# Turning the attention weights in two halves of query rows, in the attention loop of a graph network kernel

## The reference

```
q = (x @ Wq + bq).reshape(n, heads, C)      # heads = 2, C = 64
k = (x @ Wk + bk).reshape(n, heads, C)
v = (x @ Wv + bv).reshape(n, heads, C)
alpha = sum(q[dst] * k[src], axis=-1) / sqrt(C)
ex = exp(alpha - segment_max(alpha, dst)[dst])
a = ex / segment_sum(ex, dst)[dst]
out = segment_sum(v[src] * a[..., None], dst).reshape(n, heads * C)
return out + x @ Ws + bs
```

## Time and profile before

| | us |
|---|---|
| median of three runs | 2256.75 |
| the profiled execution, time | 2258.27 |
| the profiled execution, span | 2256.3 |
| TensorE busy | 2103.7 (93% of the span) |
| VectorE busy | 1578.7 (70%) |
| ScalarE busy | 1292.8 (57%) |

### The profile page before, as it was taken

How to read it: one execution, slowest core, us unless ns; L and a number is a source line. 1 busy time by engine, 2 the same in 40 slices (tenths; PEclk the granted TensorE clock), 3 DMA queues, 4 the chain that set the end, 5 groups by cost and what they waited for, 6 DMA issues and landing times. The chain is left out here.

```text
span 2256.3 us, 55086 instructions
## 1 busy us (share of the span) xinstructions
PE 2103.7 (93%) x19640; PEld 1706.4 (76%) x19640; DVE 1578.7 (70%) x4061; ACT 1292.8 (57%) x2303; POOL 834.2 (37%) x1091
## 2 busy tenths in 40 slices
PE   1299999999999999999997999999999999999998
PEld 1288888898888888988885677777776577777776
DVE  1457888888788887887773666666664666667665
ACT  1166666665666666666663455656654455655555
POOL 0765777677667767776730000000000000000000
PEclk9599999999999999999998999999999999999999
DMA  4001111111111111111112122222220222222220
GB/s 121 14 31 46 42 46 51 42 42 46 54 40 46 45 51 39 50 50 44 40 45 98 66 79 86 85 85 85 85 85 33 86 92 93 92 92 92 92 92 7
DMA packets 52537, 141.55 MB, mean 63 GB/s; under 512 B 9261, under 2 KB 43755, under 8 KB 45855
## 3 DMA queue, kind: packets, MB, share of 16 engines
q1 hardware_dynamic: 49804, 129.55, 16.2%
q0 software_dynamic: 2576, 9.68, 1.6%
HBM read 93.95 MB, written 45.27 MB: 62 GB/s over the span
## 5 line engine op out<-in xcount | busy, mean ns | idle before, releaser
L776 PE MATMUL ps<-matrixT,x_rows 125*128 125x256 f32 (+1 forms) x2500 | 581.6, 383 | 2.8 <-ACT aggT L862 2.1
L843 ACT COPY matrixT<-ps 125x500 f32<-125x500 f32 (+2 forms) x800 | 395.7, 582 | 224.7 <-PE ps L764 220.7
L776 PEld LDWEIGHTS ps<-matrixT,x_rows 125*128 125x128 f32 x2500 | 459.8, 190 | 71.3 <-issue 3.2
L1466 ACT COPY weightsT_l<-ps 125x500 f32<-125x500 f32 (+1 forms) x450 | 234.0, 543 | 368.9 <-PE ps L1387 368.9
L764 PE MATMUL ps<-high_weights,low_onehot 64*125 64x125 f32 x6300 | 404.6, 279 | 23.6 <-issue 11.7
L1544 DVE CUSTOM_DVE_ANT_0 scores_l<-ps,bias_rows_l 125x500 f32<-125x500 f32 (+1 forms) x700 | 396.8, 619 | 35.3 <-issue 33.7
L764 PEld LDWEIGHTS ps<-high_weights,low_onehot 64*125 64x125 f32 x6300 | 367.0, 189 | 53.5 <-issue 31.9
L1387 PEld LDWEIGHTS ps<-eye,scores_l 125*125 125x125 f32 x2500 | 301.0, 189 | 115.7 <-issue 97.3
L1387 PE MATMUL ps<-eye,scores_l 125*125 125x125 f32 x2500 | 364.1, 286 | 4.7 <-ACT scores_l L1448 3.4
L1552 DVE COPY weightsT_l<-ps 125x500 f32<-125x500 f32 (+1 forms) x250 | 150.0, 600 | 267.3 <-PE ps L1387 264.9
L1448 ACT ACTIVATE scores_l<-scores_l,neg_max_l 125x1500 f32<-125x1500 f32 x200 | 320.9, 1605 | 20.5 <-DVE neg_max_l L1581 20.2
(11 more groups left out here) (154 smaller groups left out, 2028.1 us busy)
## 6 DMA issues: line engine op xcount, KB each, us to landing
bias_rows_l<-bias SPq DMA_DIRECT2D x50, 1562.5 KB, 6.6
bias<-bias SPq DMA_DIRECT2D x150, 250.0 KB, 2.0
edges<-rec POOLq DMA_DIRECT2D x1, 2014.2 KB, 11.8
x_rows<-in_x SPq DMA_DIRECT2D x1, 1562.5 KB
bias<-bias SPq DMA_DIRECT2D x25, 62.5 KB, 1.6
x<-x_rows SPq DMA_DIRECT2D x25, 62.5 KB
x_rows_l<-x SPq DMA_DIRECT2D x25, 62.5 KB
out<-rows_l SPq DMA_DIRECT2D x25, 62.5 KB
```

The source lines that it names most:

```text
L776: last = nc.tensor.matmul(psG[:, BASES * SPLIT * side:BASES * (SPLIT * side + SIDE[side])], x[:, h, :], MT[side][:, 0:SIDE[side], BASES * ...
L843: last = nc.scalar.copy(MT[side][:, at:at + 2 * c - 1:2, 0:COLS], psP[bank][0:R, :].rearrange("p (i c) -> p i c", c=128)[:, 0:c, 0:COLS])
L1466: nc.scalar.copy(PT[i % 8][:, 0:cw[c]], psT[i % 2][0:R, 0:cw[c]]).then_inc(z["pa_ok"], 1)
```

## The change

`turn` now handles a chunk of both heads in one call. Each block of 125 query rows by 125 source nodes is transposed in two parts: rows 0 to 63 (`QS[0]`, 64 rows) into bank `psT[0]`, rows 64 to 124 (61 rows) into bank `psT[1]`. A full chunk is 16 transposes in place of 8. The first of each chunk is written as a matmul with the identity and not as a transpose. A bank holds both heads of a chunk (8 parts of 64 or of 61 columns). The copies now take one bank each: i = 2c + side in place of 2c + head, still on the same engines, and they wait on one count of `t_ps` per chunk. The eight `PT` tiles of one head become four of both heads. Lines 1405 and 1406 (1420 and 1421 in the changed kernel) move ahead of the turn of chunk 2s-2, so that they come straight behind the products.

```
         QS = ((0, HD), (HD, R))

-            def turn(u, up, i):
-                c, hd = i // HEADS, i % HEADS
+            def turn(u, up, c):
                 if c in (0, EXP_AT):
-                    pe.wait_ge(z["exp_ok"], u * 4 + (hd + 1 + 2 * (c > 0)))
-                if i >= 2:
-                    chunk_out(pe, u, i - 2)
-                elif not is_int(u) or u >= 1:
-                    chunk_out(pe, u - 1, i - 2 + NT)
-                for b in range(cw[c] // R):
-                    n = 4 * c + b
-                    last = nc.tensor.transpose(psT[i % 2][0:R, b * R:(b + 1) * R], S[up][:, hd, n * R:(n + 1) * R],
-                                               eye[0:R, 0:R])
+                    pe.wait_ge(z["exp_ok"], u * 4 + (2 if c == 0 else 4))
+                for i in (HEADS * c - 2, HEADS * c - 1):
+                    if i >= 0:
+                        chunk_out(pe, u, i)
+                    elif not is_int(u) or u >= 1:
+                        chunk_out(pe, u - 1, i + NT)
+                k = cw[c] // R
+                for hd in range(HEADS):
+                    for b in range(k):
+                        at = (4 * c + b) * R
+                        for side, (lo, hi) in enumerate(QS):
+                            n = hi - lo
+                            to = psT[side][0:R, (hd * k + b) * n:(hd * k + b + 1) * n]
+                            if hd == 0 and b == 0 and side == 0:
+                                nc.tensor.matmul(to, S[up][lo:hi, hd, at:at + R], eye[lo:hi, lo:hi], start=True, stop=True)
+                            else:
+                                last = nc.tensor.transpose(to, S[up][lo:hi, hd, at:at + R], eye[lo:hi, lo:hi])
                 last.then_inc(z["t_ps"], 1)

+        def turned_chunk(eng, u, i):
+            c, (lo, hi) = i // HEADS, QS[i % HEADS]
+            k = cw[c] // R
+            eng.wait_ge(z["t_ps"], u * CH + (c + 1))
+            buffer_free(eng, u, i)
+            return (PT[c % 4][:, :, 0:k, lo:hi],
+                    psT[i % HEADS][0:R, 0:HEADS * k * (hi - lo)].rearrange("p (h b q) -> p h b q", h=HEADS, b=k))
...
-                                                PT[(HEADS * c + hd) % 8][:, b * R:(b + 1) * R],
+                                                PT[c % 4][:, hd, b, :],
```

More of the change, by code:

```diff
@@ L1239, in conv @@
         S = [sb(f"scores{i}", [R, HEADS, NODES], F32) for i in range(2)]
-        PT = [sb(f"weightsT{i}", [R, CW], F32) for i in range(8)]
+        PT = [sb(f"weightsT{i}", [R, HEADS, 4, R], F32) for i in range(4)]
         mx = [sb(f"chunk_max{i}", [R, HEADS, CH], F32) for i in range(2)]
@@ L1267, in conv @@
         EXP_BEFORE = {2: 2, 4: 3}
+        QS = ((0, HD), (HD, R))
         EXP_AT = 3
@@ L1398, in step @@
                         product(w, par, CH - 1)
-                    if s > 0 and inside(u):
-                        turn(u, up, 4 * s - 4)
-                        turn(u, up, 4 * s - 3)
                     if s == 2 and inside(w):
@@ L1406, in step @@
                         nc.tensor.matmul(psO[par][0:R, 384:384 + D], x_now[par][:, :], W["s"][:, :], start=True, stop=True).then_inc(z["o_ps"], 1)
+                    if s > 0 and inside(u):
+                        turn(u, up, 2 * s - 2)
                     if s > 0 and inside(t):
@@ L1411, in step @@
                     if s > 0 and inside(u):
-                        turn(u, up, 4 * s - 2)
-                        turn(u, up, 4 * s - 1)
+                        turn(u, up, 2 * s - 1)
                         if s == 1 and (not is_int(u) or u >= 2):
@@ L1422, in step @@
                 if inside(u):
-                    turn(u, up, NT - 2)
-                    turn(u, up, NT - 1)
+                    turn(u, up, CH - 1)
             pipeline_loop(pe, step)
@@ L1462, in step @@
                             continue
[L1463 to L1466, removed]
+                        to, turned_rows = turned_chunk(act, u, i)
+                        nc.scalar.copy(to, turned_rows).then_inc(z["pa_ok"], 1)
                         if layer == 1 and i == 12 and inside(w):
@@ L1535, in step @@
                     if not is_int(t) or t >= 2:
-                        v.wait_ge(z["t_ps"], (t - 1) * NT)
+                        v.wait_ge(z["t_ps"], (t - 1) * CH)
                         v.wait_ge(z["neg_ok"], t - 1)
@@ L1548, in turned_out @@
                 def turned_out(i):
[L1549 to L1552, removed]
+                    to, turned_rows = turned_chunk(v, u, i)
+                    V.tensor_copy(to, turned_rows).then_inc(z["pt"], 1)
                 if inside(t):
```

## The result

| | before | changed |
|---|---|---|
| median | 2257.01 us (4 runs) | 2336.45 us (4 runs, 2332.09 to 2337.53) |
| profiled execution, time / span | 2258.27 / 2256.3 us | 2337.53 / 2335.5 us |
| mean granted clock of TensorE | 0.981 | 0.971 |

The changed kernel is slower: the ratio is 1.0345, with a 95% interval of 1.0333 to 1.0358.

The account below looks back on a forecast made before the run. TensorE, never idle in a 19.23 us step, was taken as the bound. Savings, extra slots and waits gave +1.43 and +1.14 us a step, times 25 each +64: 2322, or 2321 against the median, range 2295 to 2350.

Parts of the forecast that it names:

- A slot of two halves costs what a whole turn costs (0.109): TensorE's turns: two halves side by side stay at 0.109 us, because each still loads 125 weight columns.
- Rival 1: Turn slots: the load is not the limit, halves are twice as fast, slot 0.060, total 2181 us; chance 0.19.
- rival 2: Turn slots: transposes in halves do not overlap, slot 0.218, +6.2 us a step, total 2632; chance 0.07.
- Plain first halves, 7 slots, +0.76: Each chunk's first half, a plain two-pass matmul, makes 57 slots a step for 50: +0.76 us.
- Halves and scores stand side by side without a change, -0.95 and -1.14: TensorE's shape changes fall from 15 to 10 in layer 1, 9 in layer 2: 0.95 and 1.14 us saved.
- Rival 3: Halves and scores remain separate kinds, so the 0.95 and 1.14 us come back: total 2373; chance 0.09.
- Waits at the products of chunks 1 and 3, 0.37 each: These products wait on TensorE for two ScalarE copies that start behind the last half: 0.37 us, twice, 0.74 a step.
- Rival 4: The new waits are half as long, since copies start sooner: total 2282 us; chance 0.09.
- Wait at the turn of chunk 5, 0.78: This turn waits for VectorE's copy, with only the narrow scores between: 0.78 us a step.
- Exponentials, 0.10 in layer 1: Turn of chunk 0 needs both heads' exponentials: a 0.10 us wait in layer 1; layer 2 keeps some spare.
- The sum a step: All gains and waits together make a step longer by 1.43 us in layer 1 and 1.14 in layer 2.
- Times 25 each: +64: From step to launch: the step losses of layers 1 and 2 are each multiplied by 25, giving +64 us.

Follow-up runs that it names:

- e4: Changed kernel, every half using only its first 32 rows and 32 moving columns, still 125 weight columns: 2427.11 us, ratio 1.0745.
- e5: Changed kernel, every half except the first of each chunk loading 64 weight columns in place of 125: 2216.20 us, ratio 0.9814.
- e3: Changed kernel, each chunk's first half a transpose too, its waits taken by an added semaphore instruction: 2301.04 us, ratio 1.0191.
- e8: Kernel before with whole turns, products issued later and lines 1405 and 1406 moved behind the products: 2264.17 us, ratio 1.0023.
- e7: Changed kernel with products issued later and a transpose as each chunk's first half: 2231.02 us, ratio 0.9875 against the kernel before.
- e2: Kernel before with only lines 1405 and 1406 moved ahead of the turns of chunk 2: 2259.09 us, ratio 1.0001.
- e9: Changed kernel plus three unused matmul pairs of the scores' shape in each layer's last turned block: 2327.09 us, ratio 1.0299.
- e1: Kernel before, whole turns, with the changed kernel's waits: one count per chunk, both heads' waits ahead of head 0. 2328.70 us, ratio 1.0308.
- e10: Changed kernel with later products, a transpose as each chunk's first half, and unused matmuls at the layers' ends: 2238.68 us, ratio 0.9899.
- e6: Changed kernel with each chunk's products issued a group later, other work between turns and products: 2265.55 us, ratio 1.0033.

## Why the prediction was right, and where its sum was short

The forecast was slower, 2321 with 2295 to 2350 around it; it came out at 2336.45. Its steps one by one:

- *A slot of two halves costs what a whole turn costs (0.109).* Right. In the changed kernel 1533.51 to 1534.27 (1533.51 + 1.03 - 0.27) are 7 slots: 0.109. That the load and not the stream sets it was an argument from the earlier trace rows then; e4 and e5 show it. Rival 1 needed a slot of 0.060, which the runs show only with 64 columns of weights (0.055 in e5); rival 2 needed 0.218. The Trainium skill's page "TensorEngine Tiling (Array Packing)", section "Theoretical Speedup", gives up to 2x; here that doubling went into two parts per slot, of which each did half of a whole turn's work. The Trainium skill's page "TensorE: Matmul & The Clock Gate", section "LDWEIGHTS (loading the stationary operand)", gives columns divided by 1.2 in ns, an estimated 104 ns for 125 columns and 53 for 64; the slots of the changed kernel (109 ns) and of e5 (55) agree. The halves' records were to be near 0.22 and are 0.27; this changed nothing in the sum, since ScalarE's copy still starts 0.32 behind the last half (1530.39, then 1530.71), for 0.33 forecast.
- *Plain first halves, 7 slots, +0.76.* Right in kind; taking them out gave back 0.57 and 0.65 a step. The missing 0.19 and 0.11 are longer waits elsewhere in e3's step, as shown there.
- *Halves and scores stand side by side without a change, -0.95 and -1.14.* Right, and a little small. The scores at 1534.28 follow the last half at once, and from halves to scores in e3 likewise. Where halves follow products, the start is 0.20 behind the last pair (1537.13 + 2.31 - 0.27 = 1539.17, then 1539.37), 0.09 more than a slot as before; but the first record is only 0.05 longer than the others (0.32 and 0.27), where a whole turn's is 0.10 longer. At four entries a step that is 0.2 more saved than forecast. From e8 to e7 it shows as 0.82 and 1.14; the later order there puts one more product between scores and halves, which takes back some 0.19. Rival 3 is out.
- *Waits at the products of chunks 1 and 3, 0.37 each.* Exact: 2.31 for 1.94, twice. Rival 4 (half as long) is out.
- *Wait at the turn of chunk 5, 0.78.* Measured 1.13 less two slots of scores and one lone pass (0.21 + 0.11): 0.81. VectorE's copy runs from 1540.61 to 1541.30, 0.32 to 1.01 behind the start of the last half (1540.29) where 0.26 to 0.94 was forecast, and the turn starts at 1.14 for 1.10.
- *Exponentials, 0.10 in layer 1.* Near: 0.04. The last product pair starts at 1526.57, so an unhindered turn would begin at 1526.77; it begins at 1526.81.
- *The sums' move costs nothing.* Right: e2.
- *The sum a step.* Forecast +1.43 and +1.14, measured +1.26 and +1.04; the 0.2 above explains most of it.

The sum was 15 us short all the same. The step that failed is the one that carried a step's loss to the total, "Times 25 each: +64": it took every block for a full step and the clock for unchanged. The ends of the layers hold the three turned blocks of each layer that are not in full steps: at the forecast's rate 3 x (1.43 + 1.14) = 7.7 us, measured 25.3. Add 4.8 for the stretches inside the loops: 22.4 us that had no term. Against it stand the cheaper steps (31.5 + 25.1 forecast, 27.6 + 22.9 measured: -6.1) and the start (-1.4): +14.9.

Most of the 17.6 us too much at the ends is the clock. With unused matmuls between the halves (e9) it stays at 1.00 in the last blocks, the same two ends are 12.6 us shorter in the profile, and the whole launch 9.4. About 5 us are left. They are at least in part waits that only the last block has: with no scores left to stand between, the turns of chunks 1 and 3 also wait for the copies of the chunk before, against the forecast's "Turns of chunks 1, 2, 3 ... No wait". In layer 2:

```profile
2307.88 0.44 PE L1404 MATMUL ps<-eye,scores_l 64*125 64x64 f32 x1 [0.86 <-DVE weightsT_l L1563]
...
2316.45 0.29 PE L1404 MATMUL ps<-eye,scores_l 64*125 64x64 f32 x1 [0.86 <-DVE weightsT_l L1563]
```

What makes the clock fall at the ends stays open. The halves are not needed for it: e1 has whole turns and 0.82 and 0.90 there. Waits of 0.77 to 0.97 us ahead of turns stand in the last blocks of the changed kernel, e1 and e7, and the kernel before has none over 0.48. But e8 has one of 0.83 and stays at 1.00, and in e10, where the filler takes the place of such waits, the clock is lower still. The stretches of 3.4 us stay open too. They stand in the changed kernel, in e3 (at 1357.0 and 1933.8) and in e9 (at 1401.5, 2050.0 and 2213.8), which have halves and waits both; in the kernel before, e1, e2, e6, e7, e8 and e10 the loops are at 1.00. In the 3.4 us before 1584.0 TensorE was busy for 2.80 at a clock of 1.00. The DMA share of 0.94 at 1584.0 is not enough by itself, since one step earlier the clock was at 1.00 with a share of 0.96:

```profile
1563.40:1566.80 3.40, 3.40 (x44) 2.77 (x42) 0.91 (x2) 2.86 (x6) 0.00 (x0) 1.00 0.96 324
```

The pieces in whole launches, from experiments: the waits +70 (e1 +69.4; e6 gives back 71), the plain first halves +35 (e3), the rest of the change, with waits present, -28 (e1 against e3). Together +77, and 2336.4 - 2259.3 is 77; the three are differences along one chain of kernels, so that they add up proves nothing. The -28 is smaller than the 49 of free steps. A full step is shorter by 0.53 in layer 1 (20.53 to 20.00) and by 0.85 in layer 2 (20.47 to 19.62), where e8 to e7 has 0.82 and 1.14. Without e7's extra product between scores and halves the latter would be an estimated 1.01 and 1.33 (0.19 more). Against that, the wait at the turn of chunk 5 grows from 0.51 in e1 (0.92 - 0.41) to 0.93 in e3 (1.14 - 0.21), which leaves 0.59 and 0.91: where TensorE waits anyway, time saved ahead of the wait is only more waiting. Over 44 full steps 0.53 and 0.85 are 30 us, and e3's two stretches at 1.2 GHz take back 3.

## What to carry to other kernels

Where the busiest engine never waits, a change of a signal's grain (one count per chunk in place of one per head) is paid in full at each place where the consumer follows at once: look in the trace for the distance between the end of the producer's group and the first reader, and put other work between them first. Here that alone turned +3.5% into +0.3% (e6), and with the plain first halves gone as well into -1.25% (e7). Splitting the turns over the array's rows gained nothing in the slot, since each part loads as many weight columns as the whole; its gain was in standing beside work of the same shape. And multiply a step's difference only by the steps that look like it: the layers' ends have other neighbours and may have another clock.

## What the runs showed of the hardware

- A pair of row halves with 125 weight columns takes 0.109 us with 64, 61 or 32 moving columns (changed kernel, e4), and 0.055 with 64 weight columns (e5).
- Behind work of another shape the first record of the halves is 0.05 us longer than the next (0.32 and 0.27) and that of whole turns 0.10 (0.373 and 0.273), with 125 weight columns both. It is not a matter of row halves as such: the scores, 64 rows and 125 weight columns, have 0.10 as well (0.682 and 0.579).
- Plain matmuls and transposes of the same row halves follow each other without a gap (a plain pass at 1533.51, transposes from 1533.51 on, the scores at 1534.28).
- TensorE can be over 85% busy and be granted 0.60 or 0.70 (the layers' ends of the changed kernel), and 98% busy and be granted 0.69 (e10). The same place was at 1.00 before (whole turns, few waits), and at 0.82 and 0.90 with whole turns and the new waits (e1). In e4, whose halves are the shortest, the mean over the launch fell to 0.945.
- The kernel with the better steps can have the lower clock: e7 has 49 us by steps over e8 and 33 by totals, with 30 us more at 1.2 GHz.
